# Two blocks of Gram products per block of degree products, and 51 instead of 24 scans among the one-hots, in the edge stage of a graph and attention kernel

## The reference, cut to what matters

```
xn = layernorm(x)
theta_x = (xn[dst] - xn[src]) @ theta_w.T + theta_b
phi_x   = xn[src] @ phi_w.T + phi_b
e   = relu(theta_x + phi_x)
out = segment_max(e, dst)                        # first graph part
q, k, v = split(xn @ w_qkv + b_qkv)              # 4 heads
attn = softmax(einsum('bhnd,bhne->bhde', k * scale, v))
x = x + out + xn + xf + mlp(layernorm(xn + xf))  # xf = attn applied to q
```

## Time and profile before

| | us |
|---|---|
| time before, median of 3 runs | 2143.66 (2143.13 to 2148.64) |
| time of the profiled execution | 2143.48 |
| span of the profiled execution | 2141.7 |
| DVE busy in the span | 1209.6 (56%) |
| PE busy in the span | 1633.4 (76%) |
| POOL busy in the span | 1120.6 (52%) |
| POOL's gathers of this stage (line 283), busy | 495.9 in 400 |
| first and last gather issued | 54.2 and 682.9 |

### The profile page before, as it was taken

How to read it: one execution, slowest core, us unless ns; L and a number is a source line. 1 busy time by engine, 2 the same in 40 slices (tenths; PEclk the granted TensorE clock), 3 DMA queues, 4 the chain that set the end, 5 groups by cost and what they waited for, 6 DMA issues and landing times. The chain is left out here.

```text
span 2141.7 us, 24015 instructions
## 1 busy us (share of the span) xinstructions
PE 1633.4 (76%) x7942; PEld 973.9 (45%) x7942; DVE 1209.6 (56%) x2735; ACT 550.3 (26%) x851; POOL 1120.6 (52%) x890
## 2 busy tenths in 40 slices
PE   7994655354634685999999967649998998999277
PEld 6971222121211463555555446525556556555155
DVE  6877867666776455777777755414553213344611
ACT  4001111101100124666666634301111001000042
POOL 0768888888886787888888878710000000000065
PEclk9556878687776666999999977769999999999589
DMA  6356788878787522221112010054423454475121
GB/s 182 81 138 178 212 223 220 221 217 223 212 220 194 127 55 42 36 35 32 35 31 35 5 41 2 2 127 107 108 70 85 125 130 114 119 188 145 53 66 28
DMA packets 200467, 239.11 MB, mean 112 GB/s; under 512 B 69342, under 2 KB 177257, under 8 KB 195121
## 3 DMA queue, kind: packets, MB, share of 16 engines
q1 hardware_dynamic: 128463, 177.63, 31.6%
q0 software_dynamic: 71920, 60.43, 12.6%
HBM read 150.80 MB, written 86.24 MB: 111 GB/s over the span
## 5 line engine op out<-in xcount | busy, mean ns | idle before, releaser
L717 POOL DMA_INDIRECT adjacency<-all_cell_val,all_cell_idx x400 | 529.7, 1324 | 132.5 <-issue 121.3
L283 POOL DMA_INDIRECT edge_ring<-b_rows,all_src_idx x400 | 495.9, 1240 | 186.7 <-issue 170.2
L1593 PE MATMUL bank<-sage_adj,w_zh 125*128 125x448 f16 x1050 | 370.1, 352 | 0.4 <-DMA sage_adj<-adjacency 0.4
L1593 PE MATMUL bank<-sage_adj,w_zl 125*128 125x448 f16 x1050 | 369.9, 352 | 0.0
L1939 POOL DMA_INDIRECT ffn_rows<-x_rows,ffn_idx x13 | 15.8, 1214 | 639.5 <-DVE ffn_idx L1828 635.8
L537 DVE SCALAR_TENSOR_TENSOR edge_ring<-edge_ring,w_keep 125x256 f32<-125x256 f32 x399 | 192.7, 483 | 129.1 <-DMA edge_ring<-b_rows,all_src_idx 108.4
L1089 ACT ACTIVATE bank<-bank,w_shift,w_scale 128x448 f32<-128x448 f32 x224 | 146.9, 696 | 76.8 <-PE bank L730 76.8
L1593 PEld LDWEIGHTS bank<-sage_adj,w_zl 125*128 125x128 f16 x1050 | 102.7, 98 | 99.2 <-issue 5.8
L1593 PEld LDWEIGHTS bank<-sage_adj,w_zh 125*128 125x128 f16 x1050 | 102.6, 98 | 97.9 <-issue 3.9
L692 DVE SCALAR_TENSOR_TENSOR edge_junk<-bank,all_key_c,all_later 125x400 f16<-125x400 f32 x232 | 145.5, 627 | 0.0
L730 PE MATMUL bank<-all_yn,w_W1h 128*128 (+1 forms) x448 | 122.8, 356 | 11.9 <-DVEq L1125 11.9
(11 more groups left out here) (463 smaller groups left out, 3173.4 us busy)
## 6 DMA issues: line engine op xcount, KB each, us to landing
sage_adj<-adjacency SPq DMA_DIRECT2D x105, 490.0 KB
run_max<-edge_ring SPq DMA_DIRECT2D x40, 1120.0 KB
adjacency<-edge_zero SPq DMA_DIRECT2D x25, 714.0 KB
experts_gb<-gate_rows SPq DMA_DIRECT2D x56, 224.0 KB, 3.3
edge_ring<-b_rows,all_src_idx POOLq DMA_INDIRECT x400, 6.7
adjacency<-all_cell_val,all_cell_idx POOLq DMA_INDIRECT x400, 2.7
sage_adj<-adjacency SPq DMA_DIRECT2D x105, 56.9 KB
run_max<-edge_ring SPq DMA_DIRECT2D x40, 130.0 KB
```

Of the source, the lines that this page charges most:

```text
L283: nc.gpsimd.indirect_dma_start(ring[:, k % RING, :], None, dram.rows[:, :], bass.IndirectOffsetOnAxis(ap=c.src_idx[:, k:k + 1], axis=0)).t ...
L717: nc.gpsimd.indirect_dma_start(dram.adj_flat, bass.IndirectOffsetOnAxis(ap=c.cell_idx[:, k:k + 1], axis=0), c.cell_val[:, k:k + 1], None). ...
L1593: ins = mm(ps[4 * b + h][:, 0:T], z[:, g * JG + j, half(h)], adj[g][:, j, :], start=(g == 0 and j == 0 and z is zh), stop=False)
```

## The change

PE now does two Gram blocks per block of degree products until the Grams are done (12 blocks of degrees among them), and then the other 13 blocks of degrees. DVE scans three columns after each group from the fifth to the thirteenth, and two after each later one: 51 scans instead of 24. The four later runs of scans shrink from 6, 8, 6 and 16 to 2, 3, 2 and 2. All instructions are the same in kind and number; only their order is another.

```
+    scans_by = lambda g: 3 * max(g - 4, 0) if g < 13 else 27 + 2 * (g - 13)
...
                 for j in range(NB):
                     grams(j)
+                    if j % 2:
+                        degrees(j // 2)
+                for j in range(NB // 2, NB):
                     degrees(j)
...
                     cells(g)
-                    if g >= 13:
-                        scan(2 * (g - 13))
-                        scan(2 * (g - 13) + 1)
+                    for k in range(scans_by(g), scans_by(g + 1)):
+                        scan(k)
...
-                for k in range(24, 30):
+                for k in range(scans_by(NH), 53):
...
-                for k in range(30, 38):
+                for k in range(53, 56):
...
-                for k in range(38, 44):
+                for k in range(56, 58):
...
-                for k in range(44, SCANS):
+                for k in range(58, SCANS):
                     scan(k)
```

## The result

The changed kernel took 2135.28 us (median of 5 runs, 2133.40 to 2137.04) beside 2143.66 for the kernel before; the ratio is 0.9954, with a 95% interval of 0.9939 to 0.9968. That is 6.9 to 13.1 us less at 2143.66; the two medians are 8.4 us apart. The profiled execution took 2133.4 us with a span of 2131.5, so 10.2 less than before. The forecast was 2129.8.

What follows compares the result with a forecast made beforehand. POOL's stream of 400 gathers was taken to bound the kernel from about 130 us to the barrier; 2143.48 - 12.7 - 1.0 = 2129.8 us, own range 2127 to 2133, stated range 2125.5 to 2138.

Steps and rivals of the forecast that it cites:

- rival of a new wait for scans: At gather 110 or another tenth, waiting for scans replaces waiting for Grams: 4 to 8 us given back, 2134 to 2138; chance 0.08.
- The term of -12.7: POOL's real waits for Gram blocks at gathers 44 to 49 all go: between 12.6 and 12.8 us saved.
- The term of -1.0 for shorter gathers: Gathers beside the tail's dense scan runs (158 to 183 us) get shorter: 1.0 us saved, bounds 0 and 1.5.
- The rival that the slowing moves with the scans: Gathers slow down wherever scans now stand, so shorter gathers save 0 instead of 1.0 us: 2130.8 us; chance 0.20.
- The base of the sum: The time of the kernel before from which the savings were subtracted: 2143.48 us.
- The loop of the one-hots: PE sets the first half's pace at 5.97 us a group, DVE the second's; degrees end at 158 instead of 142.98.
- a bound for the whole first half: If PE ran its denser first half at 2.4 GHz, DVE alone would bound the loop; degrees end at some 145 us.
- The tail: From degrees' end to line 626: 38.8 us less 12.5 for scans that leave, ending at 184.3, 2.5 us later than before.
- the five scans in front of line 364's products: Scans 8 down to 3 in the tail only filled a wait for these products, so removing them saves nothing.
- Margins: Slack before gathers wait: 8 us for Grams at gather 49, 29 at least for scans in the loop, 13 at gather 110.
- The account of the ring: Each tenth gather from 50 on wants ten columns scanned and stored; gather 110 wants scans 60 to 69, landed at 210.
- The moved scans: 27 scans move into the one-hot loop, since gather 50 and each tenth after it want ten columns scanned and stored.

Runs made afterwards that it cites:

- pe_order_only: Kernel before with only TensorE's new order of Gram and degrees blocks, scans left in their old places: 2138.55 us, ratio 0.9966.
- scans_only: Changed kernel with TensorE alternating one Gram and one degrees block as before, so only the scans' places are new: 2152.61 us, ratio 1.0033.

## Why the prediction was right, and where it was off

The mechanism was right: POOL bounds the stage, 12.6 us of it were waits for Gram blocks, they all went, and nothing took their place. The time was less well met. 2135.28 lies in the stated range of 2125.5 to 2138, but 2.3 us outside the forecast's own range of 2127 to 2133. It lies where the rival of a new wait for scans was priced (2134 to 2138), and the profile shows no such wait; the range held because it had been widened for a rival that did not come, which is in part luck.

- *The term of -12.7:* right. Idle time fell by 12.8, gather 50 stood at 130.8 (forecast 130.5), and three profiles of each kernel give 12.5 us for the stage.
- *The term of -1.0 for shorter gathers:* read in the tail's window alone and counted as if nothing stood against it. Between 158 and 183 us it is there, but most of it comes back between 120 and 158. Over 60 to 205 us the gathers' time above 1.211 us each is 2.0 to 2.2 us before and 1.7 to 2.2 after, so the term is some 0.2 instead of 1.0. The busy time of all gathers, 494.8 us on average before and 494.2 after in a spread of 3 us, can't tell. The rival that the slowing moves with the scans was the better reading of this term. The rule of the Trainium skill (GPSIMD Engine Reference, Key points), that GpSimd contends with VectorE instructions of two SBUF inputs, fits the tail, where gathers of 1.46 us come with the run of 12 scans; in the loop 126 more such instructions cost the gathers nothing that can be told.
- *The base of the sum:* it was made against 2143.48, and the 37 runs of the kernel before have a median of 2145.6. Against that the changed kernel is 10.3 us faster, where 13.7 had been forecast. The stage accounts for 12.5. The 2 us between 12.5 and 10.3 are not explained: the stretch after the barrier varies by 7 us, and the profiles show no give-back (their spans differ by 14.2 us on average).
- *The loop of the one-hots:* degrees done at 151.95, forecast 158. The paces of 5.97 and (without the high one-hot) 3.13 are as worked out, but the first one held only from about 84 us on. Until about 70 us TensorE had 2.4 GHz, which I had named as a bound for the whole first half and not taken, and DVE set the pace. The last Gram block was therefore done at 110.2 instead of 121.2, and the margin for gather 49 was 19 us instead of 8. It didn't matter for the time, since nothing there was on the path.
- *The tail:* 177.75 - 151.95 = 25.8 us long, forecast 38.8 - 12.5 = 26.3; that the five scans in front of line 364's products would save nothing shows in the wait there, 4.69 instead of 1.75.
- *Margins:* some 21 us at gather 110 instead of 13, because of the earlier tail; tested with 16 and 46 us. The account of the ring missed the one extra scan that each tenth gather waits for.
- *The moved scans:* that the new order needs them was only hinted at in the prediction; the halves show it, 5.4 us of waits without them.

## What to carry to other kernels

When one engine's stream runs through a stage without a pause, list its real waits (those above the usual issue gap) and reorder what releases them; what other engines lose is free up to their margin, and a margin can be measured by putting dead work in front of it. Try each half of a reordering alone: here one half is a gain of 7 us, the other a loss of 7, and both together a gain of 10. When work moves, a window in which it slowed a neighbour gets faster and another gets slower; compare a stretch that holds both places before making it a term of a sum.

## What was unexpected of the hardware

- 126 extra VectorE instructions with two SBUF inputs, in runs of about 3.1 us, left GpSimd's indirect gathers at their length (495.2 us for 400, against 492.9 to 496.5 in the three profiles of the changed kernel), while gathers beside the tail's scans took up to 1.47 us instead of 1.21.
- The same TensorE instructions, with the Grams two to one ahead of the degrees, had a granted clock of 0.98 to 1.00 between 58 and 70 us, against 0.54 to 0.64 in the three profiles before. The order alone gives it (1.00 in pe_order_only), the moved scans alone don't (0.60 in scans_only).
- The stages behind the barrier, with unchanged code, took 1443.0 to 1450.3 us in profiles of kernels that differ only ahead of it; differences under 5 us need many runs or a reading of the stage itself.
